# Merged terms for the first tiles, stored taps for heads 4 to 7, and a new order in a single-core attention and FFN kernel

## The reference, cut to what matters

```python
def _L0_xattn_ref(k, v, q, ssm_kernel, D, head_dim):
    kv = jnp.einsum('bhil,bhjl->bijhl', k_, v_)
    kv_f = jnp.fft.rfft(kv, n=2 * L)
    kernel_f = jnp.fft.rfft(ssm_kernel, n=2 * L)
    y = jnp.fft.irfft(kv_f * kernel_f, n=2 * L)[..., :L]
    out = y + kv * D[None, None, None, :, None]
    return jnp.einsum('bijhl,bhil->bjhl', out, q_)   # then transposed back

x = x + _L0_xattn_ref(ctx, ctx, _layernorm(x), ssm_kernel, D, 8)
x = x + _L0_ffn_ref(_layernorm(x), ...)              # silu(gate) * up, then down
```

## Time and profile before

| | |
|---|---|
| median of 3 runs | 78.2 us (78.01 to 78.25) |
| span of the profiled execution, first to last instruction | 76.7 us (its total time is not given) |
| PE busy | 70.7 us, 92% of the span |
| DVE busy | 63.9 us, 83% |
| POOL busy | 54.6 us, 71% |
| ACT busy | 46.7 us, 61% |
| DMA | 8.29 MB, nearly all of the loads within the first 25 us |

### The profile page before, as it was taken

The page is one execution under the profiler, slowest core; times in us unless marked ns, Lnnn a source line. Parts: engine busy times, 40 slices in busy tenths (PEclk is TensorE's granted clock), DMA queues, the critical chain, the costliest instruction groups (busy, mean ns, idle before and its releaser), DMA issues.

```text
span 76.7 us, 1495 instructions
## 1 busy us (share of the span) xinstructions
PE 70.7 (92%) x469; PEld 57.8 (75%) x469; DVE 63.9 (83%) x191; ACT 46.7 (61%) x115; POOL 54.6 (71%) x73
## 2 busy tenths in 40 slices
PE   4999988879999999999999999999999999999920
PEld 3767735568798777787888797988897989899810
DVE  0088399969999999899999999999999993786760
ACT  0601483275859587976868468746767798766400
POOL 5004798799889599299899949459627899939230
PEclk9999999999999999999999999999999999999995
DMA  0498999999997000000000000000000222200404
GB/s 5 132 256 279 386 344 295 285 384 397 386 353 220 13 0 0 0 0 4 4 9 0 0 0 0 0 0 0 0 9 4 68 68 68 68 9 0 137 0 137
DMA packets 7304, 8.29 MB, mean 108 GB/s; under 512 B 992, under 2 KB 6400, under 8 KB 7296
## 3 DMA queue, kind: packets, MB, share of 16 engines
q1 hardware_dynamic: 6912, 8.00, 31.7%
q10 hardware_dynamic: 384, 0.19, 0.8%
HBM read 7.12 MB, written 1.07 MB: 107 GB/s over the span
## 4 chain that ended last, share of the span: by engine, by line
PE 58%; DMA 15%; DVE 14%; SPq 3%; ACT 3%; issue 2%; DVEq 0%; ACTq 0%
PE conv L1010 18%; PE turn L957 8%; PE down L1029 8%; DMA k_ext<-ctx_ext 8%; DMA toeplitz<-taps 7%; PE conv L977 6%; PE conv L988 6%; PE conv L986 6%; DVE hidden L733 3%; DVE terms L718 2%; PE turn L939 2%; DVE terms L721 2%; PE turn L1029 2%; SPq L310 2%; ACT gate_act L508 1%
## 5 line engine op out<-in xcount | busy, mean ns | idle before, releaser
L1010 PE MATMUL conv<-f_parts,wgu 128*128 128x256 f16 x176 | 21.6, 273 | 0.3
L1010 PEld LDWEIGHTS conv<-f_parts,wgu 128*128 128x128 f16 x176 | 16.7, 98 | 3.5 <-DVE hidden L733 0.8
L376 POOL TENSOR_TENSOR products<-k_ext 128x512 f32<-128x512 f32 (+1 forms) x16 | 18.0, 1144 | 0.6 <-DMA k_ext<-ctx_ext 0.6
L508 ACT ACTIVATE gate_act<-conv,sg_sb 128x256 f32<-128x256 f32 (+1 forms) x24 | 11.2, 471 | 4.6 <-PE conv L1010 4.0
L258 POOL TENSOR_TENSOR h_lo<-hidden,h_hi 128x256 fp32r<-128x256 f32 x18 | 12.9, 729 | 1.4 <-ACT h_hi L513 1.3
L733 DVE SCALAR_TENSOR_TENSOR hidden<-conv,su_sb,gate_act 128x256 f32<-128x256 f32 (+1 forms) x24 | 11.3, 479 | 3.1 <-ACT gate_act L508 2.7
L977 PE MATMUL conv<-products,toeplitz 128*128 128x288 f32 x32 | 11.2, 434 | 0.3 <-DVE terms L725 0.3
L365 POOL TENSOR_TENSOR rstd_f<-variance_f,minus_half 128x1 f32<-128x1 f32 x8 | 5.5, 683 | 7.9 <-DVE variance_f L694 7.9
L718 DVE TENSOR_TENSOR terms<-conv,q_ext 128x512 f32<-128x512 f32 x16 | 10.8, 678 | 0.0
L986 PE MATMUL conv<-products,toeplitz 128*128 128x288 f32 x32 | 10.8, 422 | 0.0
L988 PE MATMUL conv<-products,toeplitz 128*128 128x288 f32 x32 | 10.4, 406 | 0.0
(11 more groups left out here) (64 smaller groups left out, 119.8 us busy)
## 6 DMA issues: line engine op xcount, KB each, us to landing
k_ext<-ctx_ext SPq DMA_DIRECT2D x3, 384.0 KB, 6.1
toeplitz<-taps_pad SPq DMA_DIRECT2D x2, 512.0 KB, 7.9
out<-x_sb SPq DMA_DIRECT2D x8, 128.0 KB, 1.7
toeplitz<-taps SPq DMA_DIRECT2D x3, 256.0 KB, 5.3
wg_int<-wg_t SPq DMA_DIRECT2D x1, 704.0 KB, 8.2
wu_int<-wu_t SPq DMA_DIRECT2D x1, 704.0 KB, 9.5
wd_int<-wd_t SPq DMA_DIRECT2D x1, 640.0 KB, 8.6
x_sb<-x SPq DMA_DIRECT2D x1, 512.0 KB, 7.0
```

Source lines behind the costliest of these rows:

```text
L376: nc.gpsimd.tensor_tensor(view(products[:, n:n + 1], first * MADE + GROUP, [[MADE, halves], [GROUP, 4], [1, GROUP]]), view(k, 0, [[EXT * B ...
L508: nc.scalar.activation(gate_act[up_lanes(t), i % 2, t, :], gate_of(i, t), ACT.Silu, scale=sg_sb[gate_lanes(t), t:t + 1]).then_inc(gate_act ...
L1010: done = nc.tensor.matmul(bank_of(i, t)[:, n, :], wgu[:, c, column:column + P], f_parts[:, i % 2, part, c, :], start=(c == 0 and part == 0 ...
```

## The change

- `UNMERGED` becomes 0: tiles 0 and 1 are merged once, like tile 2, with `merge_front` on POOL and `merge_back` on DVE in the lists.
- `DIRECT` becomes 4: heads 4 to 7 take their taps from `taps_pad`, in two loads of two heads; their `direct` goes from DVE's list. `load_toeplitz(4, 6)`, and with it all of SP's list behind it, waits for `taps_stored`.
- The low part of the tail chunk goes to POOL for blocks 0 to 2 (`low_ends`), with waits of POOL for its own results; the last block's stays with DVE under a semaphore of its own.
- The skip weights come as 16 columns ahead of k's head 0, in the same transfer, and for the stored taps as column 0 of `taps`; the transfers `skip_all` and `skip_sb` go.
- x of tile 1 is SP's first load, x of tiles 2 and 3 and of 4 to 7 are issued earlier; `fill` has 14 matmuls for 17; and the lists of POOL, ACT, DVE and PE are ordered anew, to the end of the kernel. The orders of ACT, and those behind the opening, are left out below.

```diff
@@ constants
-DIRECT = 8
+DIRECT = 4
-UNMERGED = 2
+UNMERGED = 0
@@ build, tensors
-k_ext = sb("k_ext", [P, H, HALVES, EXT * B])
+k_skip = sb("k_skip", [P, H + H * HALVES * EXT * B])
+skip_all = k_skip[:, 0:H]
+k_ext = k_skip[:, H:].rearrange("p (h c n) -> p h c n", h=H, c=HALVES)
...
-skip_sb = sb("skip_sb", [H, 1])
-skip_all = sb("skip_all", [P, H])
...
@@ load_k in block.sync
-        sp.dma_start(k_ext[:, first:last], ctx_ext[:, first:last]).then_inc(done, 16)
+        row = HALVES * EXT * B
+        columns = slice(H + first * row if first else 0, H + last * row)
+        sp.dma_start(k_skip[:, columns], ctx_skip[:, columns]).then_inc(done, 16)
@@ -318,36 +319,33 @@
         n = i * BLOCK_TILES + r
         sp.dma_start(out[n * P:(n + 1) * P, :], x_sb[:, n, :]).then_inc(out_stored, 16)
 
+    load_x(1, 2, x_loaded[1])
     load_k(0, 1, k_loaded[0])
     load_direct(0, 1, direct_loaded[0])
+    load_x(2, 4, x_loaded[2])
     load_k(1, 2, k_loaded[1])
     load_direct(1, 2, direct_loaded[1])
-    load_x(1, 2, x_loaded[1])
     load_k(2, 4, k_loaded[2])
     load_direct(2, 4, direct_loaded[2])
-    load_x(2, 4, x_loaded[2])
     load_k(4, 8, k_loaded[3])
-
-    sp.wait_ge(direct_loaded[1], 16)
-    load_direct(4, 6, direct_loaded[3])
-    load_direct(6, 8, direct_loaded[4])
+    load_x(4, TILES, x_loaded[3])
     sp.wait_ge(direct_loaded[2], 16)
+    sp.wait_ge(taps_stored, 16)
+    load_toeplitz(4, 6, toeplitz_loaded[0])
+    sp.dma_start(wg_int[:, :, :], wg_t.rearrange("(c p) n -> p c n", p=P)).then_inc(wg_loaded, 16)
     load_k(8, 12, k_loaded[4])
-    load_x(4, TILES, x_loaded[3])
-    sp.wait_ge(taps_stored, 16)
-    load_toeplitz(8, 12, toeplitz_loaded[0])
-    sp.dma_start(wg_int[:, :, :], wg_t.rearrange("(c p) n -> p c n", p=P)).then_inc(wg_loaded, 16)
+    load_toeplitz(6, 8, toeplitz_loaded[1])
+    sp.dma_start(su_sb[:, :], s_up).then_inc(scales_loaded, 16)
+    sp.dma_start(sg_sb[:, :], s_gate).then_inc(scales_loaded, 16)
     sp.dma_start(wu_int[:, :, :], wu_t.rearrange("(c p) n -> p c n", p=P)).then_inc(wu_loaded, 16)
-    sp.dma_start(sg_sb[:, :], s_gate).then_inc(scales_loaded, 16)
-    sp.dma_start(su_sb[:, :], s_up).then_inc(scales_loaded, 16)
     sp.dma_start(sd_sb[:, :], s_down.partition_broadcast(P)).then_inc(scales_loaded, 16)
+    load_toeplitz(8, 12, toeplitz_loaded[2])
     load_k(12, H, k_loaded[5])
-    load_toeplitz(12, H, toeplitz_loaded[1])
...
@@ block.gpsimd
-        nc.gpsimd.tensor_tensor(taps_sb[:, P:P + 1], taps_sb[:, P:P + 1], skip_sb[:, :],
+        nc.gpsimd.tensor_tensor(taps_sb[:, P:P + 1], taps_sb[:, P:P + 1], taps_sb[:, 0:1],
...
-        subtract_high(nc.gpsimd, i, t, pool_low_ready)
+        subtract_high(nc.gpsimd, i, t, tail_ready if t == FULL else pool_low_ready)
+
+    def low_ends(i):
+        low(i, FULL - 1)
+        wait(pool, pool_low_ready, low_count(i, FULL - 1))
+        low(i, FULL)
+        wait(pool, tail_ready, i + 1)
...
-    pool.wait_ge(taps_loaded, 32)
+    pool.wait_ge(taps_loaded, 16)
     add_skip_to_taps()
     pool.wait_ge(half_ready, 1)
     root_q(0)
+    root_q(1)
+    root_q(2)
+    root_q(3)
     pool.wait_ge(k_loaded[2], 16)
     pairs(2, 0, 1)
     pairs(2, 1, 2)
-    root_q(1)
     pairs(3, 0, 1)
     pairs(3, 1, 2)
     pool.wait_ge(k_loaded[3], 16)
     pairs(4, 0, 2)
-    root_q(2)
-    root_q(3)
+    merge_front(nc.gpsimd, 0)
     pairs(5, 0, 2)
     pairs(6, 0, 2)
+    merge_front(nc.gpsimd, 1)
+    root_q(4)
     pairs(7, 0, 2)
     pool.wait_ge(k_loaded[4], 16)
     pairs(8, 0, 2)
+    merge_front(nc.gpsimd, 2)
+    root_f(0)
     pairs(9, 0, 2)
-    merge_front(nc.gpsimd, 2)
-    root_q(4)
-    root_f(0)
     root_q(5)
+    root_f(1)
     pairs(10, 0, 2)
-    root_f(1)
+    root_q(6)
     pairs(11, 0, 2)
-    root_q(6)
     merge_front(nc.gpsimd, 3)
+    merge_front(nc.gpsimd, 4)
     pool.wait_ge(k_loaded[5], 16)
     pairs(12, 0, 2)
+    low(0, 0)
+    pairs(13, 0, 2)
     root_f(2)
-    pairs(13, 0, 2)
-    merge_front(nc.gpsimd, 4)
-    low(0, 0)
+    low(0, 1)
+    root_q(7)
...
-    low(0, 4)
+    low_ends(0)
     root_f(4)
...
@@ block.scalar
-    act.dma_start(skip_all[:, :], skip.rearrange("h a -> (h a)").partition_broadcast(P)).then_inc(skip_loaded, 16)
     act.dma_start(x_sb[:, 0, :], x[0:P, :]).then_inc(x_loaded[0], 16)
     act.dma_start(taps_sb[:, :], taps).then_inc(taps_loaded, 16)
-    act.dma_start(skip_sb[:, :], skip).then_inc(taps_loaded, 16)
     nc.scalar.preload_act_table(ACT.Silu)
     act.wait_ge(taps_ready, 1)
     act.dma_start(taps_pad, taps_sb[:, :]).then_inc(taps_stored, 16)
     norm_q(0)
+    evict_q(0)
+    norm_q(1)
+    norm_q(2)
     act.wait_ge(k_loaded[2], 16)
     squares(2)
-    evict_q(0)
     squares(3)
-    norm_q(1)
     act.wait_ge(k_loaded[3], 16)
     squares(4)
+    evict_q(1)
     squares(5)
     squares(6)
+    norm_q(3)
+    wrap(0)
+    evict_q(2)
+    wrap(1)
+    evict_q(3)
+    convert_gate()
     squares(7)
-    evict_q(1)
+    norm_q(4)
+    wrap(2)
     act.wait_ge(k_loaded[4], 16)
     squares(8)
-    norm_q(2)
-    wrap(0)
-    evict_q(2)
...
@@ block.vector
     def low(i, t):
-        subtract_high(dve, i, t, tail_ready if t == FULL else dve_low_ready)
+        subtract_high(dve, i, t, last_tail_ready if t == FULL else dve_low_ready)
...
     dve.memset(zeros[:, :], 0.0).then_inc(zeros_ready, 1)
+    dve.wait_ge(x_loaded[0], 16)
+    stats_of_q(0)
+    dve.wait_ge(x_loaded[1], 16)
+    stats_of_q(1)
+    moments_of_q(0)
+    variance_of_q(0)
     dve.wait_ge(k_loaded[0], 16)
     all_products(0, 0, 1)
     all_products(0, 1, 2)
+    shift_of_q(0)
+    moments_of_q(1)
     dve.wait_ge(anti_ready, 1)
-    dve.wait_ge(skip_loaded, 16)
     dve.wait_ge(direct_loaded[0], 16)
     direct(0)
-    dve.wait_ge(x_loaded[0], 16)
-    stats_of_q(0)
-    moments_of_q(0)
+    variance_of_q(1)
+    dve.wait_ge(x_loaded[2], 16)
+    stats_of_q(2)
+    stats_of_q(3)
+    moments_of_q(2)
+    moments_of_q(3)
+    variance_of_q(2)
     dve.wait_ge(k_loaded[1], 16)
     all_products(1, 0, 1)
-    variance_of_q(0)
+    variance_of_q(3)
+    shift_of_q(1)
+    all_products(1, 1, 2)
+    shift_of_q(2)
     dve.wait_ge(direct_loaded[1], 16)
     direct(1)
-    all_products(1, 1, 2)
-    dve.wait_ge(x_loaded[1], 16)
-    stats_of_q(1)
-    shift_of_q(0)
-    moments_of_q(1)
+    shift_of_q(3)
+    multiply_terms(0)
     dve.wait_ge(direct_loaded[2], 16)
     direct(2)
-    variance_of_q(1)
     direct(3)
-    dve.wait_ge(x_loaded[2], 16)
-    stats_of_q(2)
-    moments_of_q(2)
-    shift_of_q(1)
-    multiply_terms(0)
-    stats_of_q(3)
-    variance_of_q(2)
     multiply_terms(1)
-    moments_of_q(3)
-    dve.wait_ge(direct_loaded[3], 16)
-    direct(4)
-    direct(5)
-    variance_of_q(3)
-    dve.wait_ge(direct_loaded[4], 16)
-    direct(6)
-    shift_of_q(2)
     multiply_terms(2)
+    merge_back(dve, 0)
     dve.wait_ge(x_loaded[3], 16)
     stats_of_q(4)
-    shift_of_q(3)
     multiply_terms(3)
+    moments_of_q(4)
+    add_sum(0)
     stats_of_q(5)
-    multiply_terms(4)
-    add_sum(0)
-    moments_of_q(4)
-    multiply_terms(5)
-    stats_of_q(6)
     stats_of_f(0)
     variance_of_q(4)
     moments_of_q(5)
+    stats_of_q(6)
+    merge_back(dve, 1)
     moments_of_q(6)
+    multiply_terms(4)
     moments_of_f(0)
+    shift_of_q(4)
+    multiply_terms(5)
+    add_sum(1)
     variance_of_q(5)
-    add_sum(1)
     variance_of_q(6)
+    stats_of_f(1)
     variance_of_f(0)
     merge_back(dve, 2)
-    direct(7)
-    stats_of_f(1)
-    stats_of_q(7)
-    shift_of_q(4)
     multiply_terms(6)
...
-    low(0, 5)
...
-    low(1, 5)
...
-    low(2, 5)
...
@@ convolve_across and the order in block.tensor
-            pe.wait_ge(toeplitz_loaded[n // 4 - 2], 16)
+            pe.wait_ge(toeplitz_loaded[n // 2 - 2 if n < 8 else n // 4], 16)
...
-    fill(turn[:, 0:2 * P], 17)
+    fill(turn[:, 0:2 * P], 14)
     convolve_across(0)
+    pe.wait_ge(ident_ready, 1)
+    turn_q(0, q_ready, 0)
     convolve_within(0)
     convolve_across(1)
+    turn_q(1, q_ready, 1)
     convolve_within(1)
-    pe.wait_ge(ident_ready, 1)
-    turn_q(0, q_ready, 0)
     convolve_across(2)
     convolve_within(2)
-    turn_q(1, q_ready, 1)
     convolve_across(3)
     convolve_within(3)
+    turn_q(2, q_ready, 2)
+    sum_terms(0, q_ready, 0)
+    turn_q(3, q_ready, 3)
     convolve_across(4)
     convolve_within(4)
-    turn_q(2, q_ready, 2)
-    sum_terms(0, q_ready, 0)
     convolve_across(5)
     convolve_within(5)
+    sum_terms(1, x1_ready, 1)
     convolve_across(6)
-    sum_terms(1, x1_ready, 1)
-    turn_q(3, q_ready, 3)
     convolve_within(6)
+    turn_q(4, q_ready, 4)
     convolve_across(7)
+    convolve_within(7)
     sum_terms(2, x1_ready, 2)
-    convolve_within(7)
-    turn_q(4, q_ready, 4)
     convolve(8)
     turn_f(0, x1_ready, 3)
     convolve(9)
@@ -1083,60 +1081,60 @@
     pe.wait_ge(w_ready, 1)
     gates(0, 0)
     gates(0, 1)
+    convolve(11)
+    sum_terms(3, f_ready, 2)
+    gates(0, 2)
```

(4 more changed lines are left out.)

201 lines of the change are left out of this document (96 added, 105 removed).

## The result

The changed kernel takes 81.9 us (81.73 to 82.12, 4 runs), beside 78.2 us for the kernel before on the same chip (78.01 to 78.25, 4 runs). The ratio is 1.049, with a 95% interval of 1.047 to 1.051: 3.8 us slower. The prediction was 76.9 us and its range ended at 79.0. The profiled execution took 81.9 us with a span of 80.1. In the executions behind these medians, 1.7 to 1.9 us lie around the span. The profiled execution of before, with its 76.7, was thus a longer one (the kernel before had a median span of 76.2 to 76.4 beside the experiments), and the loss of 3.8 us is all in the span.

What follows compares the result with a forecast made beforehand. Bound: late inputs in the opening, then PE and DVE together from 15.8 us. 1.2 us earlier at `multiply_terms(6)` plus 0.1 behind gave -1.3: span 75.4 plus 1.5 around it, 76.9 us; range 75.8 to 79.0.

Steps and rivals of the forecast that it cites:

- Shared ports: POOL beside DVE merges, 15.8 to 30.5 us: at most 0.5 us lost twice, making the forecast 77.4 to 77.9.
- DVE, 1.8 us lighter there, stops being the second full engine: Behind the checkpoint: tail low parts leave DVE, removing PE idle time there, worth 0.1 us.
- The total of the rest: Whole kernel without the shared-ports loss: 1.3 us saved, span 75.4, plus 1.5 around it, 76.9 us.
- checkpoint: Start of `multiply_terms(6)` on DVE, 24.33 us before: forecast 1.2 us earlier, near 23.1 (bounds 1.9 and 0.3 earlier).
- the 1.2 us that the forecast carries to the end: Lead at `multiply_terms(6)`, claimed to last because PE behind it has the same instructions and almost no idle time.
- POOL's work up to head 10: POOL from 9.3 us: pairs, front merges and roots sum to 18.4, ending at 27.7, when PE reaches head 10.
- POOL takes over: Rival, between 20 and 30 us: POOL's 2.8 us of added work exceeds its room, total 78.1; chance 0.18.
- The clock comes later: Rival, opening: fewer fills and PE idling delay the clock's rise to 2.4 GHz, total up to 79.0; chance 0.17.
- The stored taps are late: Rival, head 4 on PE: its taps land 1.9 us late, total 78.6; chance 0.07.
- Full relief: Rival: PE is the only bound and the opening costs nothing, 2.4 us saved, total 75.8; chance 0.14.

Runs made afterwards that it cites:

- e1: Kernel before plus an added final stretch timing DVE and POOL instructions alone and together; 5 additions and 3 pairs together took 6.30 us, total means nothing.
- e14: Changed kernel with each of DVE's 13 merges replaced by two one-SBUF-input statistics instructions, so it doesn't compute the reference; 77.07 us, 0.989 of the kernel before.
- e8: Kernel before with only tiles 0 and 1 merged (front merges on POOL, back merges on DVE); 81.37 us, 1.045 of the kernel before.
- e10: Changed kernel with POOL's `root_f(2)` moved to directly behind its front merge of tile 4, no wait added; 80.95 us, 1.035 of the kernel before.

## Why the prediction was wrong, point by point

- **The step that failed is the term "Shared ports": "POOL loses at most 0.5 us twice in the tight stretch, and the forecast would be 77.4 to 77.9".** It was mis-sized in three ways. It put the loss on POOL alone, where e1 shows that whichever starts second waits, DVE too (up to 1.75 us for an instruction of 0.68). It counted two new merges, where 8 of the 13 took over 1.1 us, as every merge and skip addition had to be placed anew against POOL's list. And it took its size from one front merge, in a kernel whose 11 merges on DVE all took 0.67 to 0.69 us, as none had to wait for a long instruction of POOL: the price of a collision is the rest of the other's instruction. Measured: 5.2 us on DVE's merges, 2.9 us more of POOL than its added work, 4.7 to 4.9 us in the total (e14 against the changed kernel). Two groups of the trace before held the hint: DVE's merges took 680 ns on average, so they had hardly met POOL, and the one front merge that took 505 ns over the median was such a meeting, seen and costed as a rarity.
- **"DVE, 1.8 us lighter there, stops being the second full engine": wrong for the same reason.** DVE had 25.38 of 25.5 us, and PE idled.
- **The total of the rest came out, its checkpoint did not.** With the merges' exclusion taken out, the same lists give 77.1 us for the 76.9 forecast, and a median span of 75.3 for the 75.4. (The 1.5 us around the span were 0.3 too few, as the prediction took them from the median and a longer execution.) Counts came as forecast (44 additions on PE, 8 front merges, 4 skip additions, 3 tails on POOL). The first real matmul came at 6.1 (6.0), the first terms at 9.3 (9.7), and the first gates at 29.9, half a us earlier instead of 1.2. But `multiply_terms(6)`, forecast near 23.1, came at 24.04, and at 24.11 in e14, whose merges were free; the kernel before had 24.33, 23.4 and 23.5. In the changed kernel two skip additions (0.85 together) and the two merges at 18.30 and 22.98 (1.14 each, 0.46 over) beside POOL account for more than the difference; the skip additions have two SBUF inputs too, and the sum had priced them at 0.34 each. So no profile shows the 1.2 us that the forecast carries to the end, nor where e14's 1.0 us came from, and that the totals agree is in part luck.
- **A sum of less weight:** POOL's work up to head 10 names six powers and adds five; the list has four there behind 9.3 us. It gave 27.7, and the pair ended at 28.04. PE did not wait for it.
- **The rivals.** *POOL takes over* had the right engine and the wrong mechanism: in e14 POOL does all of its added work (14.25 of the 14.7 us from 15.8 to 30.5) and the total is 77.1. *The clock comes later*: in the changed kernel the granted clock was 1.00 up to 7.1 us, 0.50 (the 1.2 GHz level) from 7.2 to 10.5 and 1.00 from 10.6, with convolution records 0.24 apart again, and DVE waited for no convolution. In e14 the granted clock reads 1.00 from 4 to 12 us, yet convolution records lay 0.48 or more apart from 5.83 to 9.3 us, and DVE's first terms waited 0.44 us for PE. The prediction had read the same from the earlier trace rows, 0.51 apart, where the clock of the earlier trace rows says 1.00: the column does not show every half-rate stretch, the records do. So this rival came true in e14 to 0.4 us at most. *The stored taps are late*: they landed near 15.3 and head 4 did not wait. *Full relief*: no. The rival that came true, slower by several us, was on my list as a caveat with a price and not as a rival with a chance; its bounds had been made from a single row.
- **The range** ended at 79.0 because its terms were added as if each engine's durations were given. They depend on the neighbours.
- **Open:** why the opening of one and the same list varies by 0.9 us (16.74, 15.82 and 15.80 at `multiply_terms(3)`); the waits that differ there are for transfers, and none of the runs held them fixed. And no order was found that keeps PE's relief and avoids the collisions: nothing run here that computes all of the reference beat the kernel before.

The Trainium skill (SBUF — State Buffer, Who interferes with whom) says it as a rule: the port pair that VectorE and GpSimd share goes to whichever instruction comes first, for its whole length, and the other blocks. A VectorE instruction with two SBUF inputs contends in this way with a GpSimd instruction that reads SBUF. One with at most one SBUF input, outside the 2-port performance modes, does not. The runs agree where the instructions are long: 1.75 us for 0.68, 0.61 apart with a PSUM input, 4.9 us in the kernel. They differ for POOL's powers of 128x1, beside which additions with two SBUF inputs lost nothing (0.63 us each in e1), and there the measurement decides. The sentence that the prediction used (GPSIMD Engine Reference, Key points) says only that they contend.

## What to carry to other kernels

POOL's long instructions and DVE's with two SBUF inputs behave as one resource: cost them in one list, by their place in time and not by their amount. Place such DVE instructions where POOL waits or does its powers, or give them a PSUM input. A tuned kernel may owe its time to that placing, so that any shift, even an earlier start, can cost more than the work it saves; the control for it is cheap, the same kernel with statistics instructions of the same length in their place. And if a row shows one long outlier, find its neighbour before you price it as rare.

## What the runs showed of the hardware

- For long instructions turns are whole and go both ways: 1.75 us for DVE's addition of 0.68, and 1.70 for POOL's pair of 1.24 (e1). POOL's power of 128x1 waits as well, 0.99 us in the changed kernel at 36.88 where it took 548 ns on average in e14, but it holds DVE up by nothing that can be seen: 0.63 us for each addition beside powers in e1.
- One SBUF input is no protection by itself: a multiplication by a constant of 128x512 float32, 0.41 us at the median, took up to 1.52 beside pairs (e1), while the 26 statistics instructions over k, with one SBUF input, never took over 0.43 in e14.
- In e8 the granted clock fell to the 1.2 GHz level at about 18.7 us. PE had idled for 2.12 us up to 17.53, and had four gaps of 0.15 to 0.35 between 8 and 12 us. The clock was 0.50 from 20 to 22 us, and convolution records lay 0.48 apart from 19.1 on. The changed kernel fell to it at 7.1 us, behind an idle time of 2.08; e10, with the same opening and 2.16, did not (convolution records 0.24 apart from 7.2 us on). Another execution of e8, at a mean granted clock of 1.0, had a span of 79.6 against the 79.2 of this one, so the fall cost nothing that can be seen.
